# Attention scores of two heads as row-tiled matmuls of contraction 64

## The chip, the cores and the metric

The kernel runs on one core of a Trainium2 chip. The metric is the device time of one execution in microseconds (us), less is better.

## What is computed

Input x has 4 sequences of 512 tokens and 1024 channels. The reference, cut to what matters here:

```python
xn = layernorm(x)
q, k, v = (rotary(xn @ Wq), rotary(xn @ Wk), xn @ Wv)      # 16 heads of 64 channels
logits = einsum('bhqd,bhkd->bhqk', q, k)                   # causal mask, divided by 8
attn = softmax(where(causal, logits, -1e9) / 8)
s = einsum('bhqk,bhkd->bhqd', attn, v).reshape(...) @ Wo
g = silu(((xn * in_scale) @ sign(weight).T) * out_scale + bias)   # a routed gate
out = x + s * g
```

All of it is float32. To keep float32 accuracy in the reduced-precision matmul type the kernel splits each operand into a high part and a rest ("hi" and "lo") and adds hi x hi, hi x lo and lo x hi.

## The kernel before, in words

The first part (`ffn_block`, up to about 217 us of the span) normalises x, stores it, and computes the gate. The rest is `attention_block`.

Attention runs in 32 steps. A step `s` projects q, k and v of one pair of heads for one sequence (`project`, 8 slices of contraction with 3 matmuls each of 128x512, so 72 matmuls a step), and works in the gaps on the pair `a = s - 1` that was projected a step earlier and on the rest of pair `s - 2`. The steps run as a loop over two of them, as two sequences share their weights; an odd step also prepares the weights of the next pair (`spare` on ScalarE, `weights_low` on GpSimd). Each engine has its own instruction stream in an order written out by hand in its `step`, and the engines meet at semaphores only.

The path of one head from q and k: VectorE multiplies and shuffles the projection (`rotate_read`, L1143 and L1144), GpSimd finishes the rotation (`rotate`), ScalarE writes the hi part (`q_high` and `k_high`, 6 activations of 64x512 a step) and VectorE the rest (`q_low` and `k_low`, 4 subtractions of 64x512 a step). TensorE computes `scores`: a tile of 128 queries against its 128, 256, 384 or 512 causal keys. The three PSUM banks of a head hold the tiles (3), (2, 0) and (1). VectorE adds the mask and takes the row maximum (`maxima`, L1172), ScalarE the exponential and its sum (`exps`, L1031), VectorE divides (`normalise`, L1178 and L1182). TensorE transposes the probabilities in 10 blocks (`prob_transposes`, L896, two banks used in turn), ScalarE and VectorE split them (`pt_hi_parts`, `pt_low_parts`, L1189), TensorE multiplies by v (`values`, L909), and the two halves of its result are added (`copy_low_half`, `merge`).

In `scores` the contraction of 128 rows is filled with both parts of one head's q: rows 0-63 hold q hi and rows 64-127 q lo (for head 1 the other way round). The keys stand twice (`k_hh`, hi in both halves), so that one matmul gives hi x hi + lo x hi (L878); a second one against `k_l0` (k lo in one half, zeros in the other) adds hi x lo (L879). A tile takes 2 matmuls with the whole array, a head 8, a step 16.

Of the kernel before, what the change touches and what calls it, by code (L numbers as in the profile page):

```python
# [12 lines left out]
P = 128  # L13
# [14 lines left out]
SCORE_BANKS = (((3, 0),), ((2, 0), (0, 384)), ((1, 0),))  # L28

PT_BANKS = (((0, 0),), ((1, 0), (3, 384)), ((2, 0),))  # L30
# [5 lines left out]
def raw(ap):  # L36

    return ap.bitcast(F32)

# [610 lines left out]
def attention_block(nc, block, io, keep, xn, xn_store, z_store, att_store, out):  # L650
# [5 lines left out]
    with ExitStack() as ctx:  # L656
# [17 lines left out]
        qk = sb("at_qk", [P, 2, 6, SEQ], F32R)  # L674
        q_st, k_hh, k_l0 = ([[qk[:, p, c + h, :] for h in range(2)] for p in range(2)] for c in (0, 2, 4))
# [31 lines left out]
        zeroed = sem("at_zeroed")  # L707
# [132 lines left out]
        def _(pe):  # L840
# [25 lines left out]
            def scores(a, h, parity):  # L866
                n = 2 * a + h
                pe.wait_ge(qk_ready, 2 * a + 2)
                if not later(a, 2):
                    pe.wait_ge(zeroed, 4)  # L870
# [11 lines left out]
            def prob_transposes(n, h, uses):  # L882
                if uses[0] == 0:
                    pe.wait_ge(normed, n + 1)
                for u in uses:
                    tiles = PT_BANKS[u]

                    if u == 2:
                        pe.wait_ge(pt_ready, 3 * n + 1)
                    elif later(n, 1):  # L890
                        pe.wait_ge(pt_ready, 3 * n - (0, 1)[u])
                    for kt, col in tiles:
# [6 lines left out]
            def values(a, n, h, parity):  # L899
# [3 lines left out]
                if later(n, 1):  # L903
                    pe.wait_ge(merged, n)
# [504 lines left out]
```

## Time and profile before

| | us |
|---|---|
| median of 3 runs (lowest, highest) | 1188.04 (1187.37, 1189.50) |
| the profiled execution, its own time | 1189.66 |
| its span, first to last instruction | 1187.4 |
| TensorE matmuls busy | 1142.3 |
| VectorE busy | 729.4 |
| ScalarE busy | 616.2 |
| GpSimd busy | 432.1 |

PE is TensorE's matmuls and PEld its weight loads; every matmul here is preceded by its own load of the stationary operand. DVE is VectorE, ACT ScalarE, POOL GpSimd. A line of a timeline gives the start and the duration; matmuls overlap, so the time that one takes of the engine is the distance from its start to the next start and not its duration. An idle time is shown in brackets with what ended it.

### The profile page before, as it was taken

To read this page: it belongs to the slowest core of one execution; us is meant where nothing else is said; L and a number is where in the kernel's file an instruction comes from. 1 tells how busy PE (TensorE), PEld (TensorE's weight loads), DVE (VectorE), ACT (ScalarE), POOL (GpSimd) and SP (SyncE) were. 2 spreads that over 40 slices of the span, in tenths; PEclk is the share of its full clock that TensorE was granted. 3 is DMA by queue.
4 is the path that set the end of the run, shared out by engine and by line. 5 is a ranking of instruction groups with operands and counts; after the bars stand their busy time and mean duration, and the time that the engine had idled before them with its cause. 6 is when DMAs were issued, how large, how long until landed. Compare 5 with 4: busy or idle time off the path is not lost.

```text
span 1187.4 us, 17857 instructions
## 1 busy us (share of the span) xinstructions
PE 1142.3 (96%) x5736; PEld 954.0 (80%) x5736; DVE 729.4 (61%) x1735; ACT 616.2 (52%) x1291; POOL 432.1 (36%) x258
## 2 busy tenths in 40 slices
PE   4699999999999999999999999999999998999998
PEld 3477777788888888888888888888888886888886
DVE  7676553357776777767767777767767777323133
ACT  5445344155666556656566466655665666322111
POOL 2526427433433424235333343342523523332220
PEclk9799999999999999999999999999999998999999
DMA  6734232302202022021460220202202025555652
GB/s 205 283 107 189 77 107 76 120 0 73 62 9 62 9 71 62 9 62 36 176 212 9 69 59 13 62 9 71 62 9 62 26 72 186 164 182 179 209 196 104
DMA packets 86983, 111.23 MB, mean 94 GB/s; under 512 B 3304, under 2 KB 68840, under 8 KB 85936
## 3 DMA queue, kind: packets, MB, share of 16 engines
q1 hardware_dynamic: 86960, 110.93, 28.7%
q8 instruction: 13, 0.21, 0.1%
q14 instruction: 10, 0.08, 0.0%
HBM read 77.37 MB, written 33.55 MB: 93 GB/s over the span
## 4 chain that ended last, share of the span: by engine, by line
PE 87%; DVE 6%; ACT 3%; POOL 2%; issue 1%; DMA 1%; SPq 0%; DVEq 0%; ACTq 0%; POOLq 0%
PE at_proj L44 17%; PE at_proj L46 17%; PE at_proj L45 17%; PE at_out L909 7%; PE at_pt L896 6%; PE ff_z_ps L264 6%; PE at_score L878 3%; PE at_score L879 3%; PE at_score L44 2%; PE at_score L45 2%; PE at_score L46 2%; PE at_proj L863 1%; POOL ff_xs_lo L601 1%; DMA w_stage<-in_L_ffn_weight_dram 1%; ACT xn_hi L365 1%
## 5 line engine op out<-in xcount | busy, mean ns | idle before, releaser
L44 PE MATMUL at_proj<-xn_hi,w_hi 128*128 128x512 f32 x896 | 363.4, 406 | 2.9 <-ACT at_v_t L1014 2.9
L46 PE MATMUL at_proj<-xn_hi,w_lo 128*128 128x512 f32 x896 | 352.0, 393 | 0.0
L45 PE MATMUL at_proj<-xn_lo,w_hi 128*128 128x512 f32 x896 | 350.8, 392 | 0.0
L46 PEld LDWEIGHTS at_proj<-xn_hi,w_lo 128*128 128x128 f32 x896 | 169.0, 189 | 37.6
L44 PEld LDWEIGHTS at_proj<-xn_hi,w_hi 128*128 128x128 f32 x896 | 169.5, 189 | 33.3 <-issue 3.3
L45 PEld LDWEIGHTS at_proj<-xn_lo,w_hi 128*128 128x128 f32 x896 | 169.8, 190 | 30.4
L1273 POOL TENSOR_TENSOR at_turning<-at_turning,rope_table 128x512 f32<-128x512 f32 x64 | 82.9, 1296 | 305.1 <-DVE at_turning L1144 305.1
L1281 POOL TENSOR_TENSOR w_lo<-w_stage,w_hi 128x1024 fp32r<-128x1024 f32 x45 | 114.5, 2559 | 162.8 <-ACT w_hi L993 162.8
L1031 ACT ACTIVATE at_prob<-at_score,at_neg_max 128x512 f32<-128x512 f32 (+3 forms) x256 | 133.4, 526 | 68.0 <-DVE at_neg_max L1172 67.6
L1040 ACT ACTIVATE at_pt_hi<-at_pt 128x512 fp32r<-128x512 f32 (+1 forms) x192 | 94.0, 524 | 101.1 <-PE at_pt L896 100.4
L1189 DVE TENSOR_TENSOR at_pt_lo<-at_pt,at_pt_hi 128x512 fp32r<-128x512 f32 (+1 forms) x192 | 111.8, 597 | 43.7 <-ACT at_pt_hi L1040 42.8
L1172 DVE CUSTOM_DVE_ANT_0 at_score<-at_score,at_causal 128x512 f32<-128x512 f32 (+3 forms) x256 | 120.7, 513 | 1.0
L896 PE MATMUL at_pt<-ident,at_prob 128*128 128x128 f32 x640 | 93.1, 277 | 4.9 <-DVE at_pt_lo L1189 2.8
L1047 ACT ACTIVATE at_low_half<-at_out 64x512 f32<-64x512 f32 x64 | 37.9, 593 | 103.5 <-PE at_out L909 102.7
L1182 DVE TENSOR_SCALAR at_prob<-at_prob,at_inv_sum 128x256 f32<-128x256 f32 (+3 forms) x256 | 84.4, 393 | 2.3
L1277 POOL TENSOR_TENSOR at_rotated<-at_turning 128x512 f32<-128x512 f32 x64 | 82.8, 1294 | 7.3 <-POOL at_turning L1273 4.5
L1006 ACT ACTIVATE at_qk<-at_rotated 64x512 fp32r<-64x512 f32 x128 | 80.4, 628 | 7.1 <-POOL at_rotated L1277 5.5
L1289 POOL TENSOR_TENSOR w_lo<-rope_table,w_hi 128x1024 fp32r<-128x1024 f32 x16 | 43.2, 2700 | 111.8 <-ACT w_hi L1060 111.8
L896 PEld LDWEIGHTS at_pt<-ident,at_prob 128*128 128x128 f32 x640 | 73.9, 142 | 10.6 <-DVE at_pt_lo L1189 4.1
L264 PE MATMUL ff_z_ps<-sign_t,ff_xs_hi 128*128 128x512 f32 x256 | 81.4, 399 | 0.8 <-POOL ff_xs_lo L601 0.7
L878 PE MATMUL at_score<-at_qk 128*128 128x512 f32 (+3 forms) x256 | 80.4, 327 | 0.0
L264 PE MATMUL ff_z_ps<-sign_t,ff_xs_lo 128*128 128x512 f32 x256 | 80.1, 394 | 0.0
(129 smaller groups left out, 1827.7 us busy)
## 6 DMA issues: line engine op xcount, KB each, us to landing
z_store<-z SPq DMA_DIRECT2D x16, 512.0 KB, 2.7
w_stage<-in_L_attn_Wq_dram SPq DMA_DIRECT2D x16, 512.0 KB, 3.8
w_stage<-in_L_attn_Wk_dram SPq DMA_DIRECT2D x16, 512.0 KB, 5.1
w_stage<-in_L_attn_Wv_dram SPq DMA_DIRECT2D x16, 512.0 KB, 6.1
att_store<-at_att_t SPq DMA_DIRECT2D x32, 256.0 KB, 2.0
rope_table<-att_store SPq DMA_DIRECT2D x16, 512.0 KB, 6.5
z<-_attn_hidden_states_dram SPq DMA_DIRECT2D x16, 512.0 KB, 4.5
at_turning<-z_store SPq DMA_DIRECT2D x16, 512.0 KB, 6.1
```

What stands on the lines that cost most here:

```text
L44: pe.matmul(out, sh, mh, start=first, stop=False)
L45: pe.matmul(out, sh, ml, start=False, stop=False)
L46: return pe.matmul(out, sl, mh, start=False, stop=final)
L264: last = pe.matmul(z_ps[n % 2][:, o, :], part[:, k, tok], keep["sign_t"][:, k, o * HALF:(o + 1) * HALF], start=(k == 0 and part is xs_hi), ...
L878: pe.matmul(out, q, k_hh[parity][h][:, 0:width], start=True, stop=False)
L896: last = pe.transpose(pt_ps[u % 2][:, dst:dst + P], prob[h][:, src:src + P], keep["ident"][:])
L1031: last = act.activation(prob[h][:, P_COL[t]:P_COL[t] + width], score_ps[bank][:, col:col + width], ACT.Exp, scale=-1.0, bias=neg_max[h][:, ...
L1040: act.activation(pt_hi[h][:, 512 * u:512 * u + PT_WIDTH[u]], pt_ps[u % 2][:, 0:PT_WIDTH[u]], ACT.Copy).then_inc(pt_high, 1)
L1172: last = dve.tensor_tensor_reduce(out=row, in0=row, in1=causal[:, (QT - 1 - t) * P:SEQ], scale=-1.0, scalar=FAR, op0=ALU.add, op1=ALU.min, ...
L1182: last = dve.tensor_scalar(part, part, inv_sum[h][:, t:t + 1], None, ALU.mult)
L1189: dve.tensor_tensor(pt_lo[h][:, cols], pt_ps[u % 2][:, 0:PT_WIDTH[u]], raw(pt_hi[h][:, cols]), ALU.subtract).then_inc(pt_ready, 1)
L1281: pool.tensor_tensor(w_lo[m][:], w_raw[m], raw(w_hi[m][:]), ALU.subtract).then_inc(w_ready[m], 1)
```

## The change

One head's contraction now fills 64 rows only. q and k keep their natural layout (`qk_hi`, `qk_lo`: head 0 on rows 0-63, head 1 on rows 64-127), so the splits of ScalarE and VectorE become one instruction of 128x512 each (`high`, `low`: 2 + 2 a step in place of 6 + 4), and the zeros and their semaphore go. `scores` is called for a unit `u` (one of the three bank contents) and does both heads in turn: three products for each, as matmuls on rows 0-63 and 64-127 alternately, into two different banks of the three. A step has 24 score matmuls in place of 16. The calls of `scores` are spread over the step, and the orders of ScalarE and VectorE follow. The number of projections, transposes and value matmuls stays.

```diff
-SCORE_BANKS = (((3, 0),), ((2, 0), (0, 384)), ((1, 0),))
+SCORE_UNITS = (((3, 0),), ((2, 0), (0, 384)), ((1, 0),))
+def score_entry(a, u, h):
+    return 6 * a + 2 * u + h
+def score_bank(u, h):
+    return (2 * u + h) % 3
+def pt_entry(a, h, u):
+    return 6 * a + 3 * h + u
+def pt_bank(h, u):
+    return (3 * h + u) % 2
...
-            def scores(a, h, parity):
-                n = 2 * a + h
-                pe.wait_ge(qk_ready, 2 * a + 2)
...
-                for bank, tiles in enumerate(SCORE_BANKS):
-                    if later(n, 1):
-                        pe.wait_ge(expd, 3 * (n - 1) + bank + 1)
-                    for t, col in tiles:
-                        width = (t + 1) * P
-                        out = score_ps[bank][:, col:col + width]
-                        q = q_st[parity][h][:, t * P:(t + 1) * P]
-                        pe.matmul(out, q, k_hh[parity][h][:, 0:width], start=True, stop=False)
-                        last = pe.matmul(out, q, k_l0[parity][h][:, 0:width], start=False, stop=True)
-                    last.then_inc(scored, 1)
+            def scores(a, u, parity):
+                if u == 0:
+                    pe.wait_ge(qk_ready, 2 * a + 2)
+                (q_hi, k_hi), (q_lo, k_lo) = qk_hi[parity], qk_lo[parity]
+                for h in range(2):
+                    if later(score_entry(a, u, h), 3):
+                        pe.wait_ge(expd, score_entry(a, u, h) - 2)
+                for t, col in SCORE_UNITS[u]:
+                    width = (t + 1) * P
+                    for n, (q, k) in enumerate(((q_hi, k_hi), (q_lo, k_hi), (q_hi, k_lo))):
+                        for h, rows in enumerate(pair_rows):
+                            last = pe.matmul(score_ps[score_bank(u, h)][:, col:col + width], q[rows, t * P:(t + 1) * P],
+                                             k[rows, 0:width], start=(n == 0), stop=(n == 2))
+                            if n == 2 and (t, col) == SCORE_UNITS[u][-1]:
+                                last.then_inc(scored, 1)
...
                 project(i, s, b, 0, range(0, KT // 2))
                 if later(s, 1):
                     v_transposes(s - 1)
+                    scores(s - 1, 0, 1 - b)
                 if later(s, 2):
-                    prob_transposes(2 * s - 3, 1, (2,))
+                    prob_transposes(s - 2, 1, (2,))
                 project(i, s, b, 0, range(KT // 2, KT))
                 if later(s, 2):
-                    values(s - 2, 2 * s - 3, 1, b)
-                if later(s, 1):
-                    scores(s - 1, 0, 1 - b)
-                project(i, s, b, 1)
+                    values(s - 2, 1, b)
                 if later(s, 1):
                     scores(s - 1, 1, 1 - b)
-                    prob_transposes(2 * s - 2, 0, (0, 1))
-                project(i, s, b, 2, range(0, KT - 3))
-                if later(s, 1):
-                    prob_transposes(2 * s - 2, 0, (2,))
-                project(i, s, b, 2, range(KT - 3, KT))
-                if later(s, 1):
-                    values(s - 1, 2 * s - 2, 0, 1 - b)
-                    prob_transposes(2 * s - 1, 1, (0, 1))
+                project(i, s, b, 1, range(0, KT // 2))
+                if later(s, 1):
+                    scores(s - 1, 2, 1 - b)
+                project(i, s, b, 1, range(KT // 2, KT))
+                project(i, s, b, 2, range(0, 2))
+                if later(s, 1):
+                    prob_transposes(s - 1, 0, (0, 1))
+                project(i, s, b, 2, range(2, 5))
+                if later(s, 1):
+                    prob_transposes(s - 1, 0, (2,))
+                project(i, s, b, 2, range(5, KT))
+                if later(s, 1):
+                    prob_transposes(s - 1, 1, (0, 1))
+                    values(s - 1, 0, 1 - b)
...
+            def high(s, b, c):
+                act.wait_ge(rot_done, 2 * s + c + 1)
+                if c == 0 and later(s, 2):
+                    act.wait_ge(scored, score_entry(s - 1, 0, 0))
+                act.activation(qk_hi[b][c], rotated[c][:], ACT.Copy).then_inc(high_done, 1)
...
+            def low(s, b, c):
+                dve.wait_ge(high_done, 2 * s + c + 1)
+                dve.tensor_tensor(qk_lo[b][c], rotated[c][:], raw(qk_hi[b][c]), ALU.subtract).then_inc(qk_ready, 1)
...
             def step(i, s, b):
+                if later(s, 2):
+                    pt_low_parts(s - 2, 1, (1,))
+                    merge(s - 2, 0, b)
                 if later(s, 1):
                     v_low(s - 1, 1 - b)
                 if later(s, 2):
-                    pt_low_parts(2 * s - 3, 1, (2,))
+                    pt_low_parts(s - 2, 1, (2,))
+                if later(s, 1):
+                    maxima(s - 1, 0)
                 rotate_read(s, 0)
                 if later(s, 2):
-                    merge(s - 2, 2 * s - 3, 1, b)
-                if later(s, 1):
-                    maxima(2 * s - 2, 0)
-                    normalise(2 * s - 2, 0)
-                q_low(s, b)
+                    merge(s - 2, 1, b)
+                if later(s, 1):
+                    maxima(s - 1, 1)
+                low(s, b, 0)
+                if later(s, 1):
+                    maxima(s - 1, 2)
+                    normalise(s - 1, 0)
                 rotate_read(s, 1)
                 if later(s, 1):
-                    maxima(2 * s - 1, 1, (0,))
-                    pt_low_parts(2 * s - 2, 0, (0,))
-                    maxima(2 * s - 1, 1, (1, 2))
-                    pt_low_parts(2 * s - 2, 0, (1, 2))
-                    normalise(2 * s - 1, 1)
-                k_low(s, b)
-                if later(s, 1):
-                    pt_low_parts(2 * s - 1, 1, (0, 1))
-                    merge(s - 1, 2 * s - 2, 0, 1 - b)
+                    normalise(s - 1, 1)
+                    pt_low_parts(s - 1, 0, (0, 1, 2))
+                low(s, b, 1)
+                if later(s, 1):
+                    pt_low_parts(s - 1, 1, (0,))
```

ScalarE's `step` is reordered in the same way: after `exps` of unit 0 come the copy of `values`, in odd steps a weight conversion, `exps` of unit 1 head 0, `high` of q, `exps` of unit 1 head 1 and of unit 2, then the first splits of the transposed probabilities and `high` of k. The part behind the loop, in which the last pair is finished between the first matmuls of the output projection, is reordered likewise.

## Rows read from the trace of the kernel before

**Rows 1.** The page, part 1: busy time of each engine, share, instructions
```profile
PE 1142.3 (96%) x5736; PEld 954.0 (80%) x5736; DVE 729.4 (61%) x1735; ACT 616.2 (52%) x1291; POOL 432.1 (36%) x258
```

**Rows 2.** Windows, one loop step; us, busy of PE, PEld, DVE, ACT, POOL, clock
```profile
597.73:621.92 24.19, 24.19 (x129) 20.77 (x129) 17.23 (x46) 15.10 (x34) 9.94 (x6) 1.00 0.74 260
```

**Rows 3.** Timeline, TensorE, scores of both heads: start us, duration us, instruction
```profile
607.07 0.45 PE L878 MATMUL at_score<-at_qk 128*128 128x512 f32 x1
607.35 0.39 PE L879 MATMUL at_score<-at_qk 128*128 128x512 f32 x1
607.58 0.34 PE L878 MATMUL at_score<-at_qk 128*128 128x384 f32 x1
...
607.93 0.22 PE L878 MATMUL at_score<-at_qk 128*128 128x128 f32 x1
607.99 0.27 PE L879 MATMUL at_score<-at_qk 128*128 128x128 f32 x1
...
608.27 0.28 PE L879 MATMUL at_score<-at_qk 128*128 128x256 f32 x1
608.39 0.39 PE L44 MATMUL at_proj<-xn_hi,w_hi 128*128 128x512 f32 x1
...
613.86 0.39 PE L878 MATMUL at_score<-at_qk 128*128 128x512 f32 x1
...
615.12 1.03 PE L896 MATMUL at_pt<-ident,at_prob 128*128 128x128 f32 x8
```

**Rows 4.** Timeline, weight loads on the way into the scores, same columns
```profile
607.01 0.19 PEld L878 LDWEIGHTS at_score<-at_qk 128*128 128x128 f32 x1
607.12 0.19 PEld L879 LDWEIGHTS at_score<-at_qk 128*128 128x128 f32 x1
```

**Rows 5.** Timeline, TensorE: four 16-row transposes between full-size matmuls
```profile
170.79 0.39 PE L264 MATMUL ff_z_ps<-sign_t,ff_xs_lo 128*128 128x512 f32 x1
171.10 0.32 PEld L229 LDWEIGHTS ff_small<-ident,ff_logit_t 16*128 16x128 f32 x4 [0.36 <-issue]
171.11 0.42 PE L229 MATMUL ff_small<-ident,ff_logit_t 16*128 16x16 f32 x4
171.45 0.73 PE L264 MATMUL ff_z_ps<-sign_t,ff_xs_hi 128*128 128x512 f32 x2
171.79 0.40 PE L264 MATMUL ff_z_ps<-sign_t,ff_xs_hi 128*128 128x512 f32 x1
```

**Rows 6.** Timeline, TensorE and VectorE: a projection's end, VectorE's work on one head
```profile
605.61 0.39 PE L46 MATMUL at_proj<-xn_hi,w_lo 128*128 128x512 f32 x1
...
606.13 0.69 DVE L1143 TENSOR_TENSOR at_turning<-at_proj,rope_table 128x512 f32<-128x512 f32 x1 [1.17 <-PE at_proj L46]
...
608.61 0.70 DVE L1172 CUSTOM_DVE_ANT_0 at_score<-at_score,at_causal 128x512 f32<-128x512 f32 x1
609.34 0.56 DVE L1172 CUSTOM_DVE_ANT_0 at_score<-at_score,at_causal 128x384 f32<-128x384 f32 x1
...
610.06 0.47 DVE L1172 CUSTOM_DVE_ANT_0 at_score<-at_score,at_causal 128x256 f32<-128x256 f32 x1
...
611.75 0.18 DVE L1178 RECIPROCAL at_inv_sum<-at_row_sum 128x4 f32<-128x4 f32 x1 [1.16 <-ACT at_prob L1031]
...
613.27 1.39 DVE L1149 TENSOR_TENSOR at_qk<-at_rotated,at_qk 64x512 fp32r<-64x512 f32 x2
614.69 0.69 DVE L1143 TENSOR_TENSOR at_turning<-at_proj,rope_table 128x512 f32<-128x512 f32 x1
...
615.94 0.70 DVE L1172 CUSTOM_DVE_ANT_0 at_score<-at_score,at_causal 128x512 f32<-128x512 f32 x1
```

**Rows 7.** Timeline, ScalarE: two exponentials of the same head
```profile
610.24 0.58 ACT L1031 ACTIVATE at_prob<-at_score,at_neg_max 128x384 f32<-128x384 f32 x1
...
611.15 0.47 ACT L1031 ACTIVATE at_prob<-at_score,at_neg_max 128x256 f32<-128x256 f32 x1
```

**Rows 8.** The page, part 5: transposes of probabilities, busy, mean, idle before them
```profile
L896 PE MATMUL at_pt<-ident,at_prob 128*128 128x128 f32 x640 | 93.1, 277 | 4.9 <-DVE at_pt_lo L1189 2.8
```

More of the change, by code:

```diff
@@ L25 @@
 PHI, PLO = 0, 1
[L28 to L30 removed]
+SCORE_UNITS = (((3, 0),), ((2, 0), (0, 384)), ((1, 0),))
+PT_UNITS = (((0, 0),), ((1, 0), (3, 384)), ((2, 0),))
 PT_WIDTH = (512, 512, 256)
@@ L672, in attention_block @@
         v_t = sb("at_v_t", [P, SEQ], F32)
-        qk = sb("at_qk", [P, 2, 6, SEQ], F32R)
-        q_st, k_hh, k_l0 = ([[qk[:, p, c + h, :] for h in range(2)] for p in range(2)] for c in (0, 2, 4))
+        qk = sb("at_qk", [P, 2, 2, 2, SEQ], F32R)
+        qk_hi, qk_lo = ([[qk[:, p, c, part, :] for c in range(2)] for p in range(2)] for part in (PHI, PLO))
         v_hl = [sb(f"at_v_hl{p}", [P, QT, 4, HEAD_DIM], F32R) for p in range(2)]
@@ L883, in prob_transposes @@
+            def prob_transposes(a, h, uses):
                 if uses[0] == 0:
-                    pe.wait_ge(normed, n + 1)
+                    pe.wait_ge(normed, 2 * a + h + 1)
                 for u in uses:
[L886 to L892, printed above, removed]
+                    if later(pt_entry(a, h, u), 2):
+                        pe.wait_ge(pt_ready, pt_entry(a, h, u) - 1)
+                    for kt, col in PT_UNITS[u]:
@@ L895, in prob_transposes, with values @@
                             dst = col + (t - kt) * P
-                            last = pe.transpose(pt_ps[u % 2][:, dst:dst + P], prob[h][:, src:src + P], keep["ident"][:])
+                            last = pe.transpose(pt_ps[pt_bank(h, u)][:, dst:dst + P], prob[h][:, src:src + P], keep["ident"][:])
                     last.then_inc(pt_tr, 1)
-            def values(a, n, h, parity):
+            def values(a, h, parity):
                 if h == 0:
                     pe.wait_ge(v_ready, a + 1)
-                pe.wait_ge(pt_ready, 3 * n + 3)
-                if later(n, 1):
-                    pe.wait_ge(merged, n)
+                pe.wait_ge(pt_ready, pt_entry(a, h, 2) + 1)
+                if later(2 * a + h, 1):
+                    pe.wait_ge(merged, 2 * a + h)
                 for kt in range(QT):
@@ L1021, in v_hi, with exps @@
                                ACT.Copy).then_inc(v_high, 1)
-            def exps(n, h, banks=(0, 1, 2)):
-                for bank in banks:
-                    tiles = SCORE_BANKS[bank]
-                    act.wait_ge(maxed, 3 * n + bank + 1)
-                    if bank == 0 and later(n, 2):
-                        act.wait_ge(pt_tr, 3 * n - 3)
-                    for t, col in tiles:
+            def exps(a, u, heads=(0, 1)):
+                for h in heads:
+                    act.wait_ge(maxed, score_entry(a, u, h) + 1)
+                    if u == 0 and later(a, 1):
+                        act.wait_ge(pt_tr, pt_entry(a - 1, h, 2) + 1)
+                    for t, col in SCORE_UNITS[u]:
@@ L1162, in v_low, with maxima @@
                                   raw(v_hl[parity][:, :, 0:4:3, :]), ALU.subtract).then_inc(v_ready, 1)
-            def maxima(n, h, banks=(0, 1, 2)):
-                for bank in banks:
-                    tiles = SCORE_BANKS[bank]
-                    dve.wait_ge(scored, 3 * n + bank + 1)
+            def maxima(a, u):
+                for h in range(2):
+                    dve.wait_ge(scored, score_entry(a, u, h) + 1)
                     dve.sem_inc(seen, 1)
                     dve.wait_ge(causal_ok, 2)
-                    for t, col in tiles:
-                        row = score_ps[bank][:, col:col + (t + 1) * P]
+                    for t, col in SCORE_UNITS[u]:
+                        row = score_ps[score_bank(u, h)][:, col:col + (t + 1) * P]
                         last = dve.tensor_tensor_reduce(out=row, in0=row, in1=causal[:, (QT - 1 - t) * P:SEQ], scale=-1.0,
@@ L1174, in maxima, with normalise @@
                     last.then_inc(maxed, 1)
-            def normalise(n, h):
-                dve.wait_ge(expd, 3 * n + 3)
+            def normalise(a, h):
+                dve.wait_ge(expd, score_entry(a, 2, h) + 1)
                 dve.reciprocal(inv_sum[h][:], row_sum[h][:]).then_inc(inverted, 1)
-                dve.wait_ge(inverted, n + 1)
+                dve.wait_ge(inverted, 2 * a + h + 1)
                 for t in (1, 0, 2, 3):
@@ L1199, in step @@
             def step(i, s, b):
+                if later(s, 2):
+                    pt_low_parts(s - 2, 1, (1,))
+                    merge(s - 2, 0, b)
                 if later(s, 1):
```

176 lines of the change are left out of this document (79 added, 97 removed).

## The prediction

> **What bounds the kernel now.** I read the page's busy times first, then the windows of single loop steps, then the timeline of one step. The page gives TensorE 1142.3 us of matmuls in a span of 1187.4 us, with VectorE and ScalarE far below [rows 1]. [...] Whatever is taken from VectorE or ScalarE is worth nothing by itself, and each 0.1 us more or less in TensorE's stream counts 32 times (the last time behind the loop). So the question is what `scores` costs in TensorE's stream before and after, and whether the new order makes TensorE wait.
>
> How to read the stream: a matmul's duration is no price, since the next one starts before it ends. The price is the distance of starts. At full clock it is 0.23 us for 512 columns (607.35 to 607.58), 0.175 for 384 (two in 607.58 to 607.93), 0.12 for 256 (608.27 to 608.39), and for 128 columns 0.06 where the next load is done [rows 3]. The weight loads start no closer than 0.11 us one behind the other (607.01, 607.12) [rows 4]; that is a floor for a run of narrow matmuls with the whole array, and it is why a 256-column one costs 0.28 together with the 128-column one ahead of it (607.99 to 608.27).
>
> **Scores before.** Head 0 takes from 607.07 to 608.39, 1.32 us, head 1 from 613.86 to 615.12, 1.26 us [rows 3]. Together 2.58 us of each step.
>
> **Scores after, the matmuls.** 24 matmuls form 12 pairs: three products for each of the four widths. No row shows two matmuls on different rows of the array, so the price of a pair is bounded from both sides. At best a pair costs what one full-size matmul of its width does: 0.23 + 0.175 + 0.12 + 0.12 = 0.645 us for the four widths. For the 128-column pair I take two starts at 0.06, the least distance that the rows show [rows 3]; a quarter of that table cannot be far off. Three products make 1.94 us. At worst nothing overlaps, and a pair costs the double, 3.87 us. I take 1.94. The reason is in the code and the rows: the two matmuls of a pair use disjoint rows, disjoint weights and different banks, and the rows show that the array already does two things at once, since a load of 0.19 us lies beside matmuls that start 0.23 apart without lengthening them [rows 3, 4]. [...]
>
> **Scores after, the switches.** The array changes from 128 rows to 64 and back around each call of `scores`, three times a step where it never did. The trace has this once per sequence in the first part, with tiles of 16 rows: a 512-column matmul starts at 170.79, and would hand over at 171.02. The next load starts only at 171.10, with nothing fetched ahead (the brackets give 0.36 us idle of the load path). Four small transposes follow from 171.11, then a load and a full-size matmul start together at 171.45, and the one behind it at 171.79, 0.34 later in place of 0.23 [rows 5]. From 170.79 to 171.79 are 1.00 us; less two normal slots (0.46) and four transposes at 0.06 to 0.085 each (0.24 to 0.34, the upper end counts the whole way to 171.45 as theirs) a round trip costs 0.20 to 0.30 us. I take 0.28, near the shorter spacing, because the gaps of about 0.08 on either side and the exposed load of 0.11 add up to that: 0.08 + 0.08 + 0.11 = 0.27. The stage differs (16 rows, not 64), so this is the weakest price and a rival hangs on it. Three round trips are 0.84 us.
>
> [...]
>
> **Sum.** 1.94 + 0.84 = 2.78 us against 2.58: 0.20 us more in each of 32 steps, 6.4 us. The pairing brings four widths three times (1.94) in place of four times (2 heads x 2 products, 2.58), and the three switches take more than that back.
>
> **Edits at nothing.** ScalarE issues 4 activations less a step and VectorE 2 subtractions less; both are hidden under a TensorE that is busy for the whole step [rows 2], and if TensorE did wait for them they would be worth up to their own length. The four memsets that go were done while the first projection waited. No DMA is added or moved, SyncE's order stays, GpSimd's stays. Projections, transposes and value matmuls keep their number and size. More alternation of the 128-column transposes with other work costs nothing that I can find, since the load floor of 0.11 is their price already.
>
> **Waits that the new order adds.** TensorE waits in order, so behind a late `expd` or `pt_ready` stands the whole stream. Two places are tight. (1) Unit 2 of the scores needs the exponentials of unit 1, head 0, as three banks are shared. From the end of `values` TensorE has unit 1 (3 x 0.295 + 0.28 = 1.17) and twelve projection matmuls (2.76) ahead of it: 3.93 us. The other side: VectorE is free 1.54 us after `values` (607.07 to 608.61, copy and merge) [rows 3, 6]; its maxima of 384 and 128 columns take 0.72 (609.34 to 610.06) [rows 6], the exponentials 0.91 (610.24 to 611.15) [rows 7], and handing over some 0.3: 3.5 us. Margin 0.4. (2) The third block of head 0's transposes needs `pt_low_parts` of its first block, which stands behind `rotate_read` of k and `normalise` of head 1. TensorE has six matmuls, eight transposes and nine matmuls between the k projection and there: 1.38 + 0.8 + 2.07 = 4.25 us (the eight by the 1.03 that they are busy, less the last one's tail) [rows 3]. VectorE needs 0.29 (slot end 605.84 to 606.13), 1.25 (614.69 to 615.94), 1.52 (611.75 to 613.27) and 0.71 (half of 613.27 to 614.69): 3.77 us [rows 6]. Margin 0.4 to 0.5. In front of it ScalarE has two more exponentials of unit 1 and those of unit 2, and VectorE the first `normalise`; counted with the same prices they are done before the k projection ends. So I expect no wait in the steady step. Behind the loop the transposes waited 4.9 us in the trace of before [rows 8]; the new order there can give that back or double it, -5 to +5 us, and I take 0.
>
> **The rivals.** (A) Cheap switches. If going between 128 and 64 rows costs less than in rows 5, the sign turns: the break-even is (2.58 - 1.94)/3 = 0.21 us per round trip. At 0.10 a step is 0.34 us shorter, 11 us in all: 1177 us; at zero 0.64, 20.5 us: 1167.5 us. For it speaks that the only switch in the trace is of another tile size, and that its lower bound, 0.20, is about the break-even. Against it, that the pattern recurs with the same distances for two more sequences and that no load was fetched ahead of a switch. (B) Loads one behind the other. If the two loads of a pair share one path at the 0.11 of rows 4, each pair but the widest costs 0.22: 3 x (0.23 + 3 x 0.22) = 2.67, with switches 3.51, 0.93 more a step, +30 us: 1218 us. If a load of half the rows takes 0.08, narrow pairs cost 0.16: 3.02, +14 us: 1202 us. For it: the floor exists with whole loads; against: the 16-row loads stand closer, four in 0.32 including the last one's full length [rows 5]. (C) The change doesn't do what it says and the two heads' matmuls run one behind the other: 6 x 0.645 + 0.84 = 4.71, 2.13 more a step, +68 us: 1256 us. (D) One of the two margins is misjudged by 0.7 us or more and TensorE waits 0.3 us or more in each step: +16 us at 0.3 with the forecast, 1204 us.
>
> **How the numbers follow.** The profiled execution took 1189.66 us (span 1187.4 and 2.3 around it), 1.6 above the median of 1188.04. The sum is 1189.66 + 6.4 = 1196.1 for it, or 1194.4 beside the median; I forecast 1194.5. With round trips of 0.20 to 0.30 and narrow pairs between 0.11 and 0.16 the likeliest case alone runs from 1187 to 1204. Chances: the forecast 0.43, (A) 0.22, (B) 0.20, (C) 0.09, (D) 0.06. The range leaves out (C) and the lower half of (A), and takes in both forms of (B) and the bounds of the tail: 1177 to 1220. A difference under 0.2%, 2.4 us, is about what a measurement of this kernel cannot tell from no change. Faster by more than that is nearly all of (A), 0.21. Within it fall the lower edge of the forecast and the upper edge of (A), 0.10. Slower is the rest, 0.69.
>
> **What would show it.** In the timeline of a step after, the two matmuls of a pair start less than 0.05 us apart and the next pair 0.23 us later for 512 columns; starts 0.23 apart throughout would show (C), and starts of loads 0.11 apart in the narrow pairs (B). The distance from the last projection matmul ahead of a unit to the second one behind it, less 0.46 and the pairs, is the round trip: 0.28 forecast, under 0.21 is (A). Unit 0 would take about 0.97 us, unit 1 1.17, unit 2 0.64. TensorE's idle time in a step stays zero; a bracket naming `at_pt_lo` or `at_prob` ahead of a transpose, or `at_prob` ahead of a score matmul, shows (D). A step would last 24.4 us. VectorE falls by the 1.39 us of two of its four 64x512 subtractions [rows 6] and ScalarE by four activations, with no effect. The prediction is wrong in its foundation if a step differs by more than what `scores` differs.

## The result

The changed kernel takes 1335.68 us (median of 4 runs, 1335.56 to 1336.71) against 1188.77 for the kernel before: a ratio of 1.124, 95% interval 1.1225 to 1.1257. It is 147 us slower, where 6 us were forecast.

The profile after: its page first (busy time of the engines, then groups of instructions with busy time, mean ns of one, and the idle time of the engine ahead of them).

```profile
PE 1200.0 (90%) x5992; PEld 959.3 (72%) x5992; DVE 821.9 (62%) x1667; ACT 536.6 (40%) x1163; POOL 417.4 (31%) x258
...
L910 PE MATMUL at_pt<-ident,at_prob 128*128 128x128 f32 x640 | 107.9, 306 | 92.0 <-DVE at_pt_lo L1197 90.0
L1190 DVE TENSOR_SCALAR at_prob<-at_prob,at_inv_sum 128x256 f32<-128x256 f32 (+3 forms) x256 | 186.0, 788 | 2.3
...
L895 PE MATMUL at_score<-at_qk 64*128 64x512 f32 (+3 forms) x768 | 85.7, 342 | 0.0
```

TensorE was busy for 96% of the span before [rows 1] and is for 90% now. The transposes of the probabilities, which had 4.9 us of idle time ahead of them in the whole run [rows 8], have 92.0, and 90.0 of it ended with `pt_low_parts` of VectorE. And one group of VectorE has doubled though nothing in it was edited: the four multiplications of `normalise` are 788 ns each in the mean here. Before, the same 256 instructions were four in 1.3 us where they are timed [rows 6]; by width their means were 313, 365, 414 and 480 ns (128 to 512 columns). The score matmuls (L895) have no idle time ahead of them.

The windows of two successive steps (from one start of v's transposes to the next; length, busy time of PE, PEld, DVE, ACT, POOL, then the clock, DMA share and GB/s):

```profile
524.36:556.19 31.83, 27.55 (x137) 22.19 (x136) 21.67 (x43) 13.71 (x31) 12.21 (x7) 0.89 0.02 8
556.19:582.43 26.24, 24.97 (x137) 20.08 (x136) 18.32 (x43) 10.66 (x28) 5.16 (x4) 1.00 0.25 70
```

A step took 24.19 us before, with TensorE busy in all of it at a granted clock of 1.00 [rows 2]. Now an odd one takes 31.83 and an even one 26.24, and in the odd one TensorE's granted clock is 0.89 in the mean. Here, in the timeline of TensorE, is the place where an odd step loses its time:

```profile
599.64 0.39 PE L65 MATMUL at_proj<-xn_hi,w_lo 128*128 128x512 f32 x1
604.32 0.69 PE L910 MATMUL at_pt<-ident,at_prob 128*128 128x128 f32 x2 [4.29 <-DVE at_pt_lo L1197]
604.66 0.78 PE L63 MATMUL at_proj<-xn_hi,w_hi 128*128 128x512 f32 x1
605.24 0.63 PE L64 MATMUL at_proj<-xn_lo,w_hi 128*128 128x512 f32 x1
...
608.65 1.71 PE L910 MATMUL at_pt<-ident,at_prob 128*128 128x128 f32 x8
...
610.44 0.39 PE L923 MATMUL at_out<-at_pt_lo,at_v_hl 128*128 128x512 f32 x1
```

The slot of the projection at 599.64 ends at 599.87; the two transposes of head 0's third block start at 604.32. Behind the 4.45 us gap the matmuls start 0.42 us apart where they were 0.23 apart (604.66 to 605.24 holds an exposed load too). The window 603.3 to 610.0 has a granted clock of 0.50, against 1.00 in 596.0 to 599.9 ahead of the gap; from the second `values` matmul at 610.44 the spacing is 0.23 again. From there back to 604.32 are 6.12 us; how long the same instructions take without the wait is measured below.

What TensorE waited for stands in the timelines of VectorE (each multiplication by itself) and GpSimd:

```profile
598.13 1.43 DVE L1190 TENSOR_SCALAR at_prob<-at_prob,at_inv_sum 128x256 f32<-128x256 f32 x1
599.47 1.36 DVE L1190 TENSOR_SCALAR at_prob<-at_prob,at_inv_sum 128x128 f32<-128x128 f32 x1
600.76 2.51 DVE L1190 TENSOR_SCALAR at_prob<-at_prob,at_inv_sum 128x384 f32<-128x384 f32 x1
603.19 0.47 DVE L1190 TENSOR_SCALAR at_prob<-at_prob,at_inv_sum 128x512 f32<-128x512 f32 x1
...
598.11 1.29 POOL L1286 TENSOR_TENSOR at_turning<-at_turning,rope_table 128x512 f32<-128x512 f32 x1 [4.41 <-DVE at_turning L1162]
599.48 1.27 POOL L1290 TENSOR_TENSOR at_rotated<-at_turning 128x512 f32<-128x512 f32 x1
600.71 2.34 POOL L1294 TENSOR_TENSOR w_lo<-w_stage,w_hi 128x1024 fp32r<-128x1024 f32 x1
```

`rotate_read` of k has just ended, and it released GpSimd's rotation. VectorE's first multiplication starts 0.02 us behind GpSimd's first and lasts 1.43 us; the second lasts as long as the second rotation instruction, the third (384 columns, about 0.4 us by itself) 2.51 us beside GpSimd's `weights_low` of 2.34 us. Only the fourth, 512 columns, has VectorE alone and takes 0.47. Up to there one instruction of VectorE ends for each one of GpSimd, at 599.56, 600.83 and 603.27 against 599.40, 600.75 and 603.05. The same thing happens earlier in the odd step, to the subtraction `low` of q, which reads both its inputs from SBUF. Beside the `weights_low` of GpSimd it takes 2.05 us, where it takes 0.69 in an even step, and it ends 0.55 us after GpSimd's instruction:

```profile
595.35 0.39 PE L65 MATMUL at_proj<-xn_hi,w_lo 128*128 128x512 f32 x1
...
591.31 2.40 POOL L1294 TENSOR_TENSOR w_lo<-w_stage,w_hi 128x1024 fp32r<-128x1024 f32 x1
...
592.21 2.05 DVE L1166 TENSOR_TENSOR at_qk<-at_rotated,at_qk 128x512 fp32r<-128x512 f32 x1 [0.84 <-ACT at_qk L1018]
...
596.69 0.69 DVE L1161 TENSOR_TENSOR at_turning<-at_proj,rope_table 128x512 f32<-128x512 f32 x1
```

So VectorE comes late to `rotate_read` of k (596.69), although the k projection's last slot ended at 595.58. In the kernel before it is GpSimd that is held, at a place where VectorE started first: the second of two subtractions that run from 589.07 to 590.46 starts at 589.77, `weights_low` starts 0.07 us behind it, and that takes 2.88 us in place of 2.40:

```profile
589.07 1.39 DVE L1149 TENSOR_TENSOR at_qk<-at_rotated,at_qk 64x512 fp32r<-64x512 f32 x2
...
589.84 2.88 POOL L1281 TENSOR_TENSOR w_lo<-w_stage,w_hi 128x1024 fp32r<-128x1024 f32 x1 [3.72 <-ACT w_hi L993]
```

### The profile page after: what moved, and what is told of

The parts are those of the page before. It is cut to its first block, busy times and chain, and to the rows that moved or that the text cites. A ratio compares the mean times of both kernels' runs of the same rounds, so it can differ in the third digit from the quotient of the medians.

```text
span 1333.6 us, 18039 instructions
## 1 busy us (share of the span) xinstructions
PE 1200.0 (90%) x5992; PEld 959.3 (72%) x5992; DVE 821.9 (62%) x1667; ACT 536.6 (40%) x1163; POOL 417.4 (31%) x258
## 4 chain that ended last, share of the span: by engine, by line
PE 67%; DVE 21%; issue 5%; ACT 3%; POOL 2%; DMA 1%; SPq 0%; DVEq 0%; ACTq 0%; POOLq 0%
PE at_proj L63 12%; DVE at_prob L1190 12%; PE at_proj L65 12%; PE at_proj L64 12%; PE at_out L923 6%; PE at_score L895 6%; PE ff_z_ps L283 5%; PE at_pt L910 5%; PE at_score L63 2%; PE at_score L64 2%; PE at_score L65 2%; DVE at_turning L1162 2%; DVE at_pt_lo L1197 1%; POOL ff_xs_lo L620 1%; PE at_proj L881 1%
## 5 line engine op out<-in xcount | busy, mean ns | idle before, releaser
L63 PE MATMUL at_proj<-xn_hi,w_hi 128*128 128x512 f32 x896 | 380.9, 425 | 3.4 <-DVE xn_lo L1240 2.5
L65 PE MATMUL at_proj<-xn_hi,w_lo 128*128 128x512 f32 x896 | 362.3, 404 | 0.0
L64 PE MATMUL at_proj<-xn_lo,w_hi 128*128 128x512 f32 x896 | 361.0, 403 | 0.0
L910 PE MATMUL at_pt<-ident,at_prob 128*128 128x128 f32 x640 | 107.9, 306 | 92.0 <-DVE at_pt_lo L1197 90.0
L1190 DVE TENSOR_SCALAR at_prob<-at_prob,at_inv_sum 128x256 f32<-128x256 f32 (+3 forms) x256 | 186.0, 788 | 2.3
L910 PEld LDWEIGHTS at_pt<-ident,at_prob 128*128 128x128 f32 x640 | 84.1, 158 | 129.2 <-DVE at_pt_lo L1197 103.8
L1294 POOL TENSOR_TENSOR w_lo<-w_stage,w_hi 128x1024 fp32r<-128x1024 f32 x45 | 107.1, 2379 | 124.3 <-ACT w_hi L1012 124.3
L1166 DVE TENSOR_TENSOR at_qk<-at_rotated,at_qk 128x512 fp32r<-128x512 f32 x64 | 65.9, 1029 | 37.2 <-ACT at_qk L1018 34.3
L895 PE MATMUL at_score<-at_qk 64*128 64x512 f32 (+3 forms) x768 | 85.7, 342 | 0.0
L923 PE MATMUL at_out<-at_pt_hi,at_v_hl 128*128 128x512 f32 (+3 forms) x256 | 79.5, 322 | 0.1
```

What stands on the lines that cost most here:

```text
L63: pe.matmul(out, sh, mh, start=first, stop=False)
L64: pe.matmul(out, sh, ml, start=False, stop=False)
L65: return pe.matmul(out, sl, mh, start=False, stop=final)
L895: last = pe.matmul(score_ps[score_bank(u, h)][:, col:col + width], q[rows, t * P:(t + 1) * P], k[rows, 0:width], start=(n == 0), stop=(n = ...
L910: last = pe.transpose(pt_ps[pt_bank(h, u)][:, dst:dst + P], prob[h][:, src:src + P], keep["ident"][:])
L923: last = pe.matmul(out_ps[:, kt * P:SEQ], v, part[h][:, cols], start=(kt == 0 and part is pt_hi), stop=(kt == QT - 1 and part is pt_lo))
```

## The experiments

All kernels are compared with the kernel before on the same chip; its median there was between 1187.1 and 1188.9 us. The experiments ran on three chips, so a difference of two experiments carries up to 2 us of that. The theory after reading the two traces was that VectorE and GpSimd hold each other up and that the time went to this and, through it, to TensorE's waits and its clock; the rivals were the row-tiled matmuls themselves, and the new order on VectorE even without GpSimd.

**norm_first.** `normalise` of head 1 goes ahead of `rotate_read` of k.

```diff
                     normalise(s - 1, 0)
+                    normalise(s - 1, 1)
                 rotate_read(s, 1)
                 if later(s, 1):
-                    normalise(s - 1, 1)
                     pt_low_parts(s - 1, 0, (0, 1, 2))
```

> Edit: in VectorE's step of the changed kernel `normalise` of head 1 moves ahead of `rotate_read` of k; nothing else. Theory: in the trace after, `normalise` of head 1 (four TENSOR_SCALAR that take 1.28 us for head 0) takes up to 5.54 us, because `rotate_read` of k just ahead of it releases GpSimd's work and the two engines hold each other up at SBUF; then `pt_low_parts` is late, TensorE idles about 4 us every second step and runs at half clock behind that. With the edit the second `normalise` should take 1.3 us too, TensorE's wait on at_pt_lo should vanish and only the price of the row-tiled scores should stay: about 0.35 to 0.41 us a step in the trace after, so 1188.8 + 32 x 0.41 = 1202 us. Rival 1, the row-tiled matmuls themselves are what slows TensorE: stays at 1336. Rival 2, the chain on VectorE is too long even without GpSimd: `normalise` takes 1.3 us but TensorE still waits, 1250 or more.

Measured: 1201.13 us, ratio 1.0103 (1.0084 to 1.0121). 134.6 of the 147 us are gone. Its timelines, VectorE, GpSimd and TensorE:

```profile
520.04 1.27 DVE L1190 TENSOR_SCALAR at_prob<-at_prob,at_inv_sum 128x256 f32<-128x256 f32 x4
...
521.44 1.27 DVE L1190 TENSOR_SCALAR at_prob<-at_prob,at_inv_sum 128x256 f32<-128x256 f32 x4
522.62 0.68 DVE L1161 TENSOR_TENSOR at_turning<-at_proj,rope_table 128x512 f32<-128x512 f32 x1
...
524.05 1.29 DVE L1197 TENSOR_TENSOR at_pt_lo<-at_pt,at_pt_hi 128x512 fp32r<-128x512 f32 x2
...
524.05 1.30 POOL L1286 TENSOR_TENSOR at_turning<-at_turning,rope_table 128x512 f32<-128x512 f32 x1 [6.98 <-DVE at_turning L1162]
...
525.65 0.38 PE L910 MATMUL at_pt<-ident,at_prob 128*128 128x128 f32 x2
...
529.08 0.40 PE L923 MATMUL at_out<-at_pt_lo,at_v_hl 128*128 128x512 f32 x1
```

Both heads take 1.3 us; GpSimd starts after them. Beside it stand now two instructions of `pt_low_parts`, which read one of their inputs from PSUM, and they are not held: 1.29 us for both, as without GpSimd (1.28 at 603.59 in the trace after). From the two transposes at 525.65 to the second `values` matmul at 529.08 are 3.43 us. After took 6.12 for the same instructions at a granted clock of 0.53, where it is 1.00 here, so the lower clock cost 2.7 us on top of the 4.45 us gap.

**pool_waits.** Nothing of VectorE's order is touched. GpSimd's rotation of k waits until both heads are normalised.

```diff
             def rotate(s, c):
                 pool.wait_ge(rot_read, 2 * s + c + 1)
+                if c == 1 and later(s, 1):
+                    pool.wait_ge(normed, 2 * s)
```

> Edit: the changed kernel with one more wait on GpSimd: the rotation of k starts only when `normalise` of head 1 is done. VectorE's, ScalarE's and TensorE's orders are those of the changed kernel. Theory (GpSimd holds `normalise` up): `normalise` of head 1 back to 1.3 us, TensorE's idle time ahead of the transposes from 92 us to under 5, time about 1202 us. Rival 1 (row-tiled matmuls) and rival 2 (VectorE's order by itself, `rotate_read` ahead of `normalise`): no gain, 1330 or more, as GpSimd's work is only later.

Measured: 1202.07 us, ratio 1.0115 (1.0091 to 1.014). Making GpSimd wait frees as much as reordering VectorE, and the idle time ahead of the transposes is 1.9 us in the whole run (92.0 in after, 3.5 in norm_first). The multiplications over the whole run are short again (one of the four shapes: count, busy us, mean ns; in the kernel after its mean is 937):

```profile
L1190 DVE TENSOR_SCALAR at_prob<-at_prob,at_inv_sum 128x384 f32<-128x384 f32 x64 | 26.6, 415 | 0.0
```

The second rival falls: the order of VectorE is that of the changed kernel, and it is no problem once GpSimd is out of the way.

**full_after.** The first rival: is it the row-tiled matmuls? The changed kernel's order with the scores of before.

```diff
-                    for n, (q, k) in enumerate(((q_hi, k_hi), (q_lo, k_hi), (q_hi, k_lo))):
-                        for h, rows in enumerate(pair_rows):
-                            last = pe.matmul(score_ps[score_bank(u, h)][:, col:col + width], q[rows, t * P:(t + 1) * P],
-                                             k[rows, 0:width], start=(n == 0), stop=(n == 2))
+                    for h in range(2):
+                        for n, k in enumerate((k_hh, k_l0)):
+                            last = pe.matmul(score_ps[score_bank(u, h)][:, col:col + width], q_st[parity][h][:, t * P:(t + 1) * P],
+                                             k[parity][h][:, 0:width], start=(n == 0), stop=(n == 1))
```

> Edit: the changed kernel with the scores of before: full-size matmuls with contraction 128 on doubled keys, two per tile and head, and the splits in 64-row pieces (4 more activations, 2 more subtractions a step); the new order of all engines stays. Theory (the order puts `normalise` beside GpSimd): it stays slow, 1310 to 1345 us, with `normalise` of head 1 still 3 to 5.5 us. Rival 1 (row-tiled matmuls are what costs): back to within 5 us of 1189.

Measured: 1364.13 us, ratio 1.1476 (1.1456 to 1.1496), a little above the range that was expected. Without any row tiling the new order is as slow or slower, so the row-tiled matmuls are not what costs. The multiplications of `normalise` are as long as in the kernel after (384 columns: mean 936 ns), and TensorE waits 105.2 us for `pt_low_parts`.

**full_norm_first.** Both edits together.

> Edit: both edits, full-size score matmuls on doubled keys as before and `normalise` of head 1 ahead of `rotate_read` of k. Theory: TensorE has the stream of before and no wait, 1189 us within 4; the difference to norm_first is the price of row tiling alone in the same order, about 0.35 to 0.41 us a step, 11 to 13 us. Rival (the spread order costs by itself): 1200 or more here too, and no difference to norm_first.

Measured: 1255.53 us, ratio 1.0559 (1.0541 to 1.0577). The theory's 1189 missed it; so did the rival, which had 1200 or more but no difference to norm_first, and the difference is 54 us. TensorE's longest waits inside the loop (us in total, times, longest):

```profile
PE at_proj L63 <- ACT at_v_t L1032: 29.6, 31, 4.2
PE at_pt L912 <- DVE at_prob L1204: 16.7, 17, 2.0
```

It waits for `v_copy` of ScalarE. The splits of k in four 64-row activations stand ahead of it there, where the changed kernel has one of 128x512. In the new order the four activations that the change saves are worth something; in the order before, `v_copy` stood between them.

**full_cheap.** This separates row tiling from the splits: full-size score matmuls on the natural layout. Its logits are not the reference's.

```diff
-                    for n, (q, k) in enumerate(((q_hi, k_hi), (q_lo, k_hi), (q_hi, k_lo))):
-                        for h, rows in enumerate(pair_rows):
-                            last = pe.matmul(..., q[rows, t * P:(t + 1) * P], k[rows, 0:width], start=(n == 0), stop=(n == 2))
+                    for h in range(2):
+                        for n, k in enumerate((k_hi, k_lo)):
+                            last = pe.matmul(..., (q_hi, q_lo)[h][:, t * P:(t + 1) * P], k[:, 0:width], start=(n == 0), stop=(n == 1))
```

> Edit: norm_first with the 24 row-tiled score matmuls of a step replaced by 16 full-size ones, two per tile and head, on the natural layout of q and k; the splits stay the cheap ones of the change. Part of the computation is changed by that: the logits are not those of the reference, as both heads are summed. All engines have the work and the order of norm_first except for TensorE's scores. Theory (row tiling costs 0.35 to 0.41 us a step, three changes of the array's rows above what the pairing saves): 1189 us, 11 to 13 below norm_first's 1201, TensorE without waits. Rival (the row-tiled scores cost nothing, and the 12 us come from the order): 1201 here too. full_norm_first differed from this in four more activations and two more subtractions a step, which stood ahead of v's copy: its 1255 us would then be those.

Measured: 1193.22 us, ratio 1.0052 (1.0033 to 1.007). Row tiling with three round trips costs 1201.1 - 1193.2 = 7.9 us, 0.25 a step (7.6 us against unpaired below, which ran on the same chip), and not the 11 to 13 expected. The new order costs too. full_cheap's time is only 4 to 6 us above the kernel before, but its step is 0.34 us longer (the table below), 11 us in 32; where the rest comes back is told under "Edits at nothing" in the next section. An odd step of full_cheap has two gaps of 0.20 and 0.22 us in TensorE's stream ahead of transposes that an even one has not. The trace names `normalise` behind the first and `pt_low_parts` behind the second: VectorE is late in the odd step, where `low` of q takes 2.05 us beside GpSimd. No run took that away by itself.

**unpaired.** The heads' matmuls no longer in turn.

```diff
-                    for n, (q, k) in enumerate(((q_hi, k_hi), (q_lo, k_hi), (q_hi, k_lo))):
-                        for h, rows in enumerate(pair_rows):
+                    for h, rows in enumerate(pair_rows):
+                        for n, (q, k) in enumerate(((q_hi, k_hi), (q_lo, k_hi), (q_hi, k_lo))):
```

> Edit: norm_first with the two loops of a tile's row-tiled matmuls exchanged: all three products of head 0, then those of head 1, in place of the heads in turn. The same 24 matmuls, loads and banks. Theory (the two heads' matmuls run at the same time only where they follow each other): up to 0.645 x 3 = 1.94 us more a step, 1201 + 62 = 1263 us, less if the last matmul of head 0 overlaps the first of head 1 (one pair in three: then a tile costs 5 slots in place of 3, +1.29 us a step, 1242 us). Rival (matmuls of different rows don't overlap, or the queue finds them wherever they stand): 1201.

Measured: 1200.85 us, ratio 1.012 (1.01 to 1.0141), the time of norm_first. The six matmuls of unit 0 still take 0.97 us from the first start to the last end, and their starts still lie two by two, 0.01 us apart:

```profile
705.49 0.97 PE L895 MATMUL at_score<-at_qk 64*128 64x512 f32 x6
```

**same_rows.** So it was open whether anything overlaps. Here both heads stand on rows 0-63; head 1's logits are therefore head 0's.

```diff
-                            last = pe.matmul(score_ps[score_bank(u, h)][:, col:col + width], q[rows, t * P:(t + 1) * P],
-                                             k[rows, 0:width], start=(n == 0), stop=(n == 2))
+                            last = pe.matmul(score_ps[score_bank(u, h)][:, col:col + width], q[pair_rows[0], t * P:(t + 1) * P],
+                                             k[pair_rows[0], 0:width], start=(n == 0), stop=(n == 2))
```

> Edit: norm_first with the score matmuls of both heads on rows 0-63 (both read head 0's q and k, so the result is not the reference's: head 1's logits are head 0's). Number, widths, banks and order of the 24 matmuls are those of norm_first. Why: exchanging the loops changed nothing, so it is open whether the matmuls overlap at all or are only cheap because they are narrow. Theory (two matmuls run at the same time because they stand on different rows, whatever their order in the queue): now they can't, each takes its slot, 3 x 0.645 = 1.94 us more a step, 1201 + 62 = 1263 us, starts 0.23 us apart for 512 columns. Rival (64-row matmuls take half the time each): 1201.

Measured: 1254.53 us, ratio 1.0567 (1.0533 to 1.0601), 53 us above norm_first. The same six matmuls:

```profile
713.04 1.65 PE L895 MATMUL at_score<-at_qk 64*128 64x512 f32 x6
```

1.65 us in place of 0.97: 0.68 more is the price of three 512-column matmuls (3 x 0.23). So the matmuls of the two heads do run at the same time where they stand on different rows, and so they do in unpaired (0.97 us too), although two matmuls stand between the two of a pair in program order. The 53 us are less than the 62 expected: a step is 1.76 us longer than norm_first's and not 1.94, in part because odd steps are no longer than even ones here (26.57 both), where norm_first's are by 0.17.

**one_trip.** If the switches are the price, fewer of them should give it back. All units in one call, with six banks: the three of scores, the two of the transposes and the output bank.

```diff
+        score_ps = score_ps + pt_ps + [out_ps]
...
-    return (2 * u + h) % 3
+    return 2 * u + h
...
                 if later(s, 2):
                     values(s - 2, 1, b)
                 if later(s, 1):
-                    scores(s - 1, 1, 1 - b)
-                project(i, s, b, 1, range(0, KT // 2))
-                if later(s, 1):
-                    scores(s - 1, 2, 1 - b)
-                project(i, s, b, 1, range(KT // 2, KT))
+                    for u in range(3):
+                        scores(s - 1, u, 1 - b)
+                project(i, s, b, 1)
```

> Edit: norm_first with the three calls of scores put together behind the values of head 1, so that the array changes its rows once a step in place of three times. The six banks are the three of scores, the two of the transposes and the output bank, which are idle then; maxima and exponentials follow. Theory (a round trip costs 0.33 to 0.38 us in the trace after): 2 x 0.35 less a step, 1201 - 22 = 1179 us, below the kernel before. Rival (the price sits in the row-tiled matmuls and not in the switches): 1201, no change. Second rival: the maxima come later, so TensorE waits for the probabilities; then 1185 or more, with idle time ahead of the transposes.

Measured: 1175.57 us (6 runs), ratio 0.9901 (0.9885 to 0.9918): 25.6 us below norm_first and 1% faster than the kernel before. Its scores in TensorE's timeline:

```profile
527.71 0.27 PE L926 MATMUL at_out<-at_pt_lo,at_v_hl 128*128 128x128 f32 x1
527.91 1.15 PE L898 MATMUL at_score<-at_qk 64*128 64x512 f32 x7
...
529.84 0.28 PE L898 MATMUL at_pt<-at_qk 64*128 64x256 f32 x1
530.04 0.50 PE L63 MATMUL at_proj<-xn_hi,w_hi 128*128 128x512 f32 x1
530.38 0.39 PE L64 MATMUL at_proj<-xn_lo,w_hi 128*128 128x512 f32 x1
```

The last `values` matmul (128 columns, slot of 0.11) hands over at 527.82; the projections are back in step at 530.38 less one slot, 530.15. That is 2.33 us for all scores, against 2.58 before [rows 3] and 1.94 + 0.35 by the prices of the trace after. So of the 11 to 13 us that one_trip gains on the kernel before, 0.25 x 32 = 8 are the scores'; most of the rest is won once, at the entrance of the loop (next section).

The length of a step, from one start of v's transposes to the next, mean of odd and even, in the middle of the loop:

| kernel | step, us | time, us |
|---|---|---|
| before | 24.19 | 1188.8 |
| after | 29.03 | 1335.7 |
| norm_first | 24.81 | 1201.1 |
| full_cheap | 24.53 | 1193.2 |
| same_rows | 26.57 | 1254.5 |
| one_trip | 23.94 | 1175.6 |

## Why the prediction was wrong

**The step that failed** is "Waits that the new order adds", check (2). It found a margin of 0.4 to 0.5 us by taking 1.52 us for `normalise` of head 1. That price was read at 611.75 to 613.27 [rows 6], where GpSimd was idle (610.3 to 616.1). The change puts `normalise` directly behind `rotate_read` of k, whose end releases GpSimd, and there the four multiplications take 5.53 us in an odd step (598.13 to 603.66, with `weights_low` behind the rotation) and about 3.45 in an even one. With this price alone the chain of 3.77 us becomes 7.8. Measured in the odd step it is 8.74, from the end of the k projection's last slot (595.35 + 0.23) to the transposes at 604.32: `rotate_read` of k starts 0.8 us later than priced, as `low` of q was held before it. TensorE's other work was priced right (4.25 us; 595.58 to 599.87 are 4.29) and could not cover it. Check (1) held, with no idle time ahead of the score matmuls. "Edits at nothing" said that GpSimd's order stays; it does, but what runs beside it does not, and I priced the moved step without asking for its neighbour. That VectorE and GpSimd hold each other up was nowhere in the rivals. The sum of the loss: in two steps 8.4 us over norm_first, of which about 4.45 + 1.4 us are gaps ahead of the transposes and 2.7 us the lower clock behind the longer one. 8.4/2 x 32 = 135 us, and norm_first gave back 134.6.

**Rival (D)** had the place right, `at_pt_lo` ahead of a transpose, and the size wrong: it was priced at 0.3 us a step, where 4.2 were measured, with a chance of 0.06. It also left out the clock, which was granted at 0.50 behind the gap of 4.45 us (603.3 to 610.0).

**Scores, the matmuls: right.** The timeline of a step after, around the three calls, then the last two pairs of unit 2 by themselves, and weight loads of the first pair and of the narrow pairs of unit 2:

```profile
614.25 0.60 PE L881 MATMUL at_proj<-ident,at_v_t 128*128 128x128 f32 x4
614.78 0.97 PE L895 MATMUL at_score<-at_qk 64*128 64x512 f32 x6
615.67 0.44 PE L910 MATMUL at_pt<-ident,at_prob 128*128 128x128 f32 x2
615.87 0.48 PE L63 MATMUL at_proj<-xn_hi,w_hi 128*128 128x512 f32 x1
616.18 0.39 PE L64 MATMUL at_proj<-xn_lo,w_hi 128*128 128x512 f32 x1
...
619.82 0.27 PE L923 MATMUL at_out<-at_pt_lo,at_v_hl 128*128 128x128 f32 x1
620.02 1.08 PE L895 MATMUL at_score<-at_qk 64*128 64x384 f32 x12
621.03 0.50 PE L63 MATMUL at_proj<-xn_hi,w_hi 128*128 128x512 f32 x1
621.37 0.39 PE L64 MATMUL at_proj<-xn_lo,w_hi 128*128 128x512 f32 x1
...
623.68 0.39 PE L65 MATMUL at_proj<-xn_hi,w_lo 128*128 128x512 f32 x1
624.00 0.62 PE L895 MATMUL at_score<-at_qk 64*128 64x256 f32 x6
624.54 0.50 PE L63 MATMUL at_proj<-xn_hi,w_hi 128*128 128x512 f32 x1
624.88 0.40 PE L64 MATMUL at_proj<-xn_lo,w_hi 128*128 128x512 f32 x1
...
624.22 0.39 PE L895 MATMUL at_score<-at_qk 64*128 64x256 f32 x4
```

```profile
614.77 0.19 PEld L895 LDWEIGHTS at_score<-at_qk 64*128 64x128 f32 x2 [0.17 <-issue]
...
624.10 0.30 PEld L895 LDWEIGHTS at_score<-at_qk 64*128 64x128 f32 x4
```

Two loads start together at 614.77, and four take 0.30 us in unit 2, a distance of 0.11 and one length of 0.19, so they start two by two. (B) is out, and same_rows rules out (C). For the columns 1.94 us fits. That a pair costs one slot was an estimate, as no row of before has such a pair; same_rows shows it, with six matmuls in 1.65 us on the same rows and 0.97 on different ones.

**Scores, the switches: right in kind, too small.** Unit 0: from 614.25 to 616.18 are 1.93 us; less four and two transposes at 0.11 and a slot of 0.23 remain 1.04 (0.97 forecast). Unit 1: 619.93 to 621.14, 1.21 (1.17). Unit 2: 623.91 to 624.65, 0.74 (0.64). Together 2.99 against 2.78. Less 0.69, 0.88 and 0.36 for the pairs, a round trip is 0.33 to 0.38 us, above both ends of the 0.20 to 0.30 that I read from a switch to 16 rows [rows 5]. My 0.27 had two gaps of 0.08 and one exposed load of 0.11; the trace has an exposed load on each side. In unit 2: a gap of 0.09 (623.91 to 624.00), the second pair 0.22 behind the first (624.00 to 624.22) in place of 0.12, a gap of 0.08 (624.46 to 624.54), and the second projection matmul 0.34 behind the first in place of 0.23, 0.38 in all. (A), cheap switches, is out. one_trip, which saves two round trips, got 25.6 / 32 = 0.80 us a step back. Of these, 0.66 stand in the scores (2.99 less 2.33), 0.33 for each trip; the rest is its other order, in which odd steps are no longer than even ones.

**Sign and foundation.** Slower was right, but for 12 of 147 us only. The sentence "a step differs by more than what `scores` differs" was the test of the foundation, and it failed. With the wait taken away the forecast of +6.4 us would still have been low: norm_first is at +12.2 to 12.4. That this is near the forecast is in part luck. Its step is 0.62 us longer than before (24.81 against 24.19) and not 0.20: about 0.28 by row tiling and 0.34 by the order, which the sum had at nothing. From the first transposes of v to the last, norm_first takes 17.7 us longer than before (766.1 against 748.4); it comes to the first ones 5.2 us earlier.

**Edits at nothing: right for the steady step of the order before only.** ScalarE's and VectorE's savings were covered by TensorE's full stream (busy in all 24.19 us of a step [rows 2]). full_norm_first shows what the four activations cost where they stand ahead of `v_copy`: 62 us against full_cheap, together with two subtractions of VectorE. And at the entrance of the loop there is no such cover. The first projection of the second step waits there for the `v_copy` of the first, 2.89 us in the kernel before and 0.78 in the one after:

```profile
235.43 0.77 PE L44 MATMUL at_proj<-xn_hi,w_hi 128*128 128x512 f32 x1 [2.89 <-ACT at_v_t L1014]
...
232.92 0.47 PE L63 MATMUL at_proj<-xn_hi,w_hi 128*128 128x512 f32 x1 [0.78 <-ACT at_v_t L1024]
```

Before, the granted clock is low behind this wait as well: 0.51 in the window 234.6 to 241.5. From the first projection of the attention part to the first transposes of v are 24.6 us before, 20.1 in after, norm_first and full_cheap, and 25.8 in full_after, which has the doubled splits and the four memsets back. So the splits and the memsets that the change saves are worth about 5 us once; which of them, no run separates. (full_cheap's profiled execution also reached its attention part 3 us earlier than that of before, at 213.1 against 216.1, which has nothing to do with its edit.)

## What to carry to other kernels

When a step is moved on one engine, ask what runs beside it in its new place, not only what stands before and behind it: the four multiplications of `normalise` took 1.3 us next to an idle GpSimd, and 5.53 and 3.45 us next to a busy one (after). VectorE instructions that work on SBUF alone, as these do, should not stand directly behind the one that releases GpSimd; `pt_low_parts`, which reads PSUM, can stand there (1.29 us for two of 512 columns, norm_first). Row tiling paid where the row-tiled matmuls stood together: two matmuls on different rows take one slot (six of 512 columns in 0.97 us, in 1.65 on the same rows), but each change of the array's rows and back costs 0.33 to 0.38 us. Here three changes a step lose 0.25 us to 16 full-size matmuls, and one change gains 0.25 (2.33 against 2.58).

## What the runs showed of the hardware that I had not expected

- VectorE's `tensor_scalar` on SBUF advanced by one instruction for each GpSimd `tensor_tensor` beside it: 1.43, 1.36 and 2.51 us beside instructions of 1.29, 1.27 and 2.34, in place of 0.28 to 0.42. The mean of GpSimd's 128x512 ones stayed at 1.29 us. In two places the one that started second was held: VectorE's subtraction of two SBUF inputs took 2.05 us in place of 0.69 where it started 0.90 behind GpSimd (after), GpSimd's `weights_low` 2.88 in place of 2.40 where it started 0.07 behind VectorE (before). `pt_low_parts`, with one input from PSUM, was not held (1.29 us for two beside GpSimd, norm_first).
- TensorE ran the matmuls of the two row halves side by side in both orders of six that were tried, in turn and three after three: six of 512 columns took 0.96 us in norm_first and 0.97 in unpaired, the whole 1201.1 and 1200.9. On the same rows it is 1.65 and 1254.5.
- A round trip from 128 rows to 64 and back cost 0.33 to 0.38 us (after): two gaps of 0.08 to 0.09 and a weight load of about 0.11 left exposed on each side.
- After a gap of 4.45 us TensorE ran its next 6.12 us at a granted clock of 0.53, 2.7 us lost on top (after); with the gap of 1.4 us in an even step the clock of the step is 1.00.
